# A graph layer and a routed expert layer on one core: the loop's squares move to ScalarE, the degree guard to a spare tile row, one-hots to five places, and the end of the routing is put in another order

## What is computed

```python
def gnn(feat, W_self, W_neigh, b, src, dst):      # feat = layernorm(x)
    agg = segment_sum(feat[src], dst, n)          # 53125 edges, sorted by dst
    deg = segment_sum(ones, dst, n)
    return feat @ W_self + (agg / max(deg, 1)) @ W_neigh + b

def ffn(x, ...):                                  # x = layernorm(x1)
    vals, idx = top_k(x @ gate_w + gate_b, 2)
    h = relu(x @ w1[e] + b1[e]); y_e = h @ w2[e] + b2[e]      # for the two experts
    return layernorm(x + sum_k softmax(vals)_k * y_idx_k) * gamma + beta

x1 = x + gnn(layernorm(x), ...)
out = x1 + ffn(layernorm(x1), ...)
```

## Time and profile before

| | us |
|---|---|
| median of 3 runs | 567.57 (565.23 to 568.28) |
| the profiled execution | 565.0 |
| its span, first to last instruction | 563.1 |

### The profile page before, as it was taken

The page is one execution under the profiler, slowest core; times in us unless marked ns, Lnnn a source line. Parts: engine busy times, 40 slices in busy tenths (PEclk is TensorE's granted clock), DMA queues, the critical chain, the costliest instruction groups (busy, mean ns, idle before and its releaser), DMA issues.

```text
span 563.1 us, 14414 instructions
## 1 busy us (share of the span) xinstructions
PE 479.7 (85%) x5119; PEld 410.8 (73%) x5119; DVE 439.1 (78%) x1090; ACT 379.5 (67%) x929; POOL 339.7 (60%) x479
## 2 busy tenths in 40 slices
PE   1899989999898998999934799999999999998820
PEld 0455568887787886888824698899999999896610
DVE  4888769999998999989865777676777777664794
ACT  1455656877775876866643588888888888877131
POOL 5672007777665677577410677777777777652383
PEclk9999989999998999999966799999999999999975
DMA  9410024444543344321130423632332222337989
GB/s 217 96 29 1 1 78 124 135 118 128 146 122 101 114 136 122 91 70 38 31 119 1 122 73 112 170 94 79 96 92 87 74 82 81 72 90 186 220 131 147
DMA packets 45077, 56.68 MB, mean 101 GB/s; under 512 B 5347, under 2 KB 37851, under 8 KB 45006
## 3 DMA queue, kind: packets, MB, share of 16 engines
q1 hardware_dynamic: 34736, 36.73, 24.3%
q0 software_dynamic: 9440, 18.28, 13.0%
q10 hardware_dynamic: 830, 0.74, 0.6%
HBM read 39.73 MB, written 17.99 MB: 102 GB/s over the span
## 4 chain that ended last, share of the span: by engine, by line
PE 49%; DVE 31%; DMA 7%; issue 5%; POOL 3%; ACT 2%; SPq 1%; DVEq 0%; ACTq 0%; POOLq 0%
PE PS L1251 13%; PE PS L1263 13%; DVE W L1405 7%; DVE W L1498 5%; PE PS L1064 4%; PE PS L1144 4%; PE PS L1145 4%; DVE oh_extra L1405 3%; PE PS L1096 3%; DMA W<-z_tab 2%; DMA arena<-xh_tab,tok_of 2%; PE PS L1239 2%; DVE AGG L1506 2%; DVE arena L1508 1%; DVE AGG L1586 1%
## 5 line engine op out<-in xcount | busy, mean ns | idle before, releaser
L1144 PE MATMUL PS<-arena,AGG 125*128 125x257 f16 x625 | 148.9, 276 | 0.0
L1145 PE MATMUL PS<-arena,AGG 125*128 125x256 f16 x625 | 148.4, 274 | 0.0
L850 ACT ACTIVATE AGG<-PS 128x500 f16<-128x500 f32 (+1 forms) x175 | 93.1, 542 | 39.6 <-PE PS L1096 36.3
L1251 PE MATMUL PS<-arena,AGG 128*128 128x128 f16 x1536 | 97.9, 221 | 1.7 <-issue 0.8
L752 POOL DMA_INDIRECT z_tab<-arena,meta_of x64 | 79.9, 1249 | 31.5 <-issue 19.5
L1263 PE MATMUL PS<-AGG,arena 128*128 128x256 f16 x768 | 95.8, 273 | 1.3 <-DVE AGG L1714 1.0
L1251 PEld LDWEIGHTS PS<-arena,AGG 128*128 128x128 f16 x1536 | 89.9, 99 | 2.9 <-DVE AGG L1708 1.6
L746 POOL DMA_INDIRECT arena<-xh_tab,tok_of x64 | 66.8, 1044 | 37.0 <-issue 17.8
L980 ACT ACTIVATE arena<-PS,arena 128x128 f32<-128x128 f32 x256 | 73.2, 369 | 10.4 <-PE PS L1251 4.0
L1263 PEld LDWEIGHTS PS<-AGG,arena 128*128 128x128 f16 x768 | 72.8, 98 | 10.1 <-DVE AGG L1714 1.2
L1405 DVE TENSOR_TENSOR W<-table,arena 128x1024 f16<-128x1024 f16 x104 | 74.7, 727 | 6.6 <-PE PS L1096 6.6
(11 more groups left out here) (243 smaller groups left out, 890.3 us busy)
## 6 DMA issues: line engine op xcount, KB each, us to landing
W<-in_L_ffn_w SPq DMA_DIRECT2D x60, 256.0 KB, 3.2
out<-AGG SPq DMA_DIRECT2D x25, 125.0 KB
xh_tab<-arena SPq DMA_DIRECT2D x25, 125.0 KB
W<-z_tab SPq DMA_DIRECT2D x2, 1344.0 KB
W<-z_tab SPq DMA_DIRECT2D x2, 896.0 KB
W<-in_x SPq DMA_DIRECT2D x2, 784.0 KB
AGG<-out SPq DMA_DIRECT2D x2, 672.0 KB
out<-W POOLq DMA_DIRECT2D x2, 672.0 KB, 6.9
```

The source lines that it names most:

```text
L850: a.activation(AT[j % 2][:, :, QT * GD * s:QT * GD * s + n * GD].rearrange("p h (g l) -> p h g l", l=GD), (p_A0[s % 2] if j == 0 else p_A[ ...
L1144: t.matmul(p_agg[j % 2], AT[j % 2][0:BT, h, :], HW[0:BT, h, D:HS - 1], start=(h == 0), stop=False)
L1145: ins = t.matmul(p_agg[j % 2][:, 0:D], AT[j % 2][0:BT, h, :], HW[0:BT, h, 0:D], start=False, stop=(h == NB - 1))
L1251: ins = t.matmul(p_h[s % 2][:, c * P:(c + 1) * P], w1e[:, s % 2, wa, k, c * P:(c + 1) * P], xT[:, s % 2, xa, k, :], start=(y == 0), stop=( ...
```

## The change

Its edits fall in four groups.

- **Squares on ScalarE.** For row blocks 0 to 22, `x1_norm` ends with the fused operation that makes x1 and also sums it (`accum_out`). GpSimd makes minus the mean from the sum. ScalarE squares x1 minus the mean with an accumulated sum (`x1_square`, new, behind evict 3 of the pass behind). GpSimd does the rest of the scale from that. Statistics and aggregate go from VectorE for these rows. ScalarE's order in a pass becomes: weight, evict 0, xt_make, evict 1, xt_high, weight, evict 2, xtT_out, evict 3, x1_square, weight, evicts 4 to 6.
- **Degree guard.** Row 125 of the count tile and of `HW` holds 2^-14 (written by GpSimd in the prologue), the degree column holds 16, and one step of the degree's product reads 126 rows. The maximum with 1 goes from `x1_norm`; its reciprocal reads PSUM.
- **Five places.** One-hots have five places up to batch 113 (the first of pass 18's block), three after. The two new ones lie where the last expert's second weights go; SyncE waits for 452 products before the load that uses that room for staging.
- **Routing end.** Row one-hots are laid out with the two choices next to each other. TensorE multiplies two chunks before it transposes the item list. ScalarE makes the last expert's high halves before it scales the last set, and VectorE their low halves before it reads the gather's result.

```diff
@@ -26,7 +26,9 @@
-ORING = 3
+ORING = 5
+ORING_LATE = 3
+SHRINK_AT = -(-BG * 18 // QT)
...
+        def hot_place(q):
+            return q % ORING if q < SHRINK_AT else (q - SHRINK_AT) % ORING_LATE
+        def hot_before(q):
+            return max([r for r in range(q) if hot_place(r) == hot_place(q)], default=-1)
@@ -598,6 +614,8 @@
+                if n + STAGES == NPIECE:
+                    sp.wait_ge(tiles_done, QT * SHRINK_AT)
@@ -691,6 +709,13 @@
+            pool.wait_ge(consts_made, 15)
+            g.memset(HW[96:P, 0, 0:2 * D], 0.0).then_inc(guarded, 1)
+            g.memset(HW[96:P, 0, 2 * D:HS], GUARD).then_inc(guarded, 1)
+            for v in range(2):
+                g.memset(AT[v][96:P, 0, 0:BT], GUARD).then_inc(guarded, 1)
+            pool.wait_ge(guarded, 4)
...
-            g.memset(HW[:, :, 2 * D:HS], 1.0).then_inc(cleared, 1)
+            g.memset(HW[0:BT, :, 2 * D:HS], WSS).then_inc(cleared, 1)
@@ -756,16 +782,18 @@
-                y, m = rstds[:, j:j + 1], mv[:, j % 2, :]
-                pool.wait_ge(mv_made, j + 1)
-                link(g.tensor_scalar(sc[0], m[:, 1:2], EPS, None, ALU.add))
+                y, nm = rstds[:, j:j + 1], x1_nmean[:, j % 2:j % 2 + 1]
+                pool.wait_ge(x1_made, j + 1)
+                g.tensor_scalar(nm, x1_sum[:, j % 2:j % 2 + 1], -1.0 / D, None, ALU.mult).then_inc(x1_mean, 1)
+                pool.wait_ge(x1_squared, j + 1)
+                link(g.tensor_scalar(sc[0], x1_sq[:, j % 2:j % 2 + 1], 1.0 / D, EPS, ALU.mult, ALU.add))
...
-                link(g.tensor_tensor(sc[1], m[:, 0:1], y, ALU.mult))
-                g.tensor_scalar(nmr[:, j % 2:j % 2 + 1], sc[1], -1.0, None, ALU.mult).then_inc(x1_scaled, 1)
+                pool.wait_ge(x1_mean, j + 1)
+                g.tensor_tensor(nmr[:, j % 2:j % 2 + 1], nm, y, ALU.mult).then_inc(x1_scaled, 1)
@@ -870,21 +898,32 @@
+            def x1_square(j):
+                act.wait_ge(x1_mean, j + 1)
+                if j >= 2:
+                    act.wait_ge(x1_scaled, j - 1)
+                    act.wait_ge(xtT_made, j)
+                    act.wait_ge(xt_lo, j - 1)
+                a.activation(xt_of(j), x1_of(j), ACT.Square, bias=x1_nmean[:, j % 2:j % 2 + 1],
+                             accum_out=x1_sq[:, j % 2:j % 2 + 1]).then_inc(x1_squared, 1)
@@ -927,18 +966,20 @@
             for i in range(NB):
-                if i >= 2:
-                    xt_make(i - 2)
                 weight_high(slot_piece(i, 0))
                 A_evict(i + 1, 0)
                 if i >= 2:
+                    xt_make(i - 2)
+                A_evict(i + 1, 1)
+                if i >= 2:
                     xt_high(i - 2)
                 weight_high(slot_piece(i, 1))
-                A_evict(i + 1, 1)
                 A_evict(i + 1, 2)
                 if i >= 2:
                     xtT_out(i - 2)
                 A_evict(i + 1, 3)
+                if 1 <= i < NB - 1:
+                    x1_square(i - 1)
...
-            scale_tokens(SETS - 1)
-            scale_blocks(SETS - 1)
             for c, (w, src_f, scale) in enumerate(((W1, wstg4, WS1), (W2, wstg3, WS2))):
                 act.wait_ge(last_loaded, 2 * DMA)
                 a.activation(w[:, NEXP - 1, 0, :, :].rearrange("p k f -> p (k f)"), src_f, ACT.Copy, scale=scale).then_inc(last_hi, 1)
+            scale_tokens(SETS - 1)
+            scale_blocks(SETS - 1)
@@ -1141,7 +1182,8 @@
-                    t.matmul(p_agg[j % 2], AT[j % 2][0:BT, h, :], HW[0:BT, h, D:HS - 1], start=(h == 0), stop=False)
+                    rows = BT + 1 if h == 0 else BT
+                    t.matmul(p_agg[j % 2], AT[j % 2][0:rows, h, :], HW[0:rows, h, D:HS - 1], start=(h == 0), stop=False)
@@ -1215,8 +1257,6 @@
-            pe.wait_ge(item_cols, 1)
-            t.transpose(p_item, scr[0:NITEM, 0:1], ident[0:NITEM, 0:NITEM]).then_inc(item_T, 1)
...
                 ins.then_inc(chunk_done, 1)
+                if c == 1:
+                    pe.wait_ge(item_cols, 1)
+                    t.transpose(p_item, scr[0:NITEM, 0:1], ident[0:NITEM, 0:NITEM]).then_inc(item_T, 1)
@@ -1399,10 +1442,10 @@
-                if q >= ORING:
-                    dve.wait_ge(tiles_done, QT * (q - ORING + 1))
+                if hot_before(q) >= 0:
+                    dve.wait_ge(tiles_done, QT * (hot_before(q) + 1))
@@ -1501,16 +1544,18 @@
-                link(v.tensor_scalar(deg[:, 0:1], p_deg[j % 2], 1.0, WSS, ALU.max, ALU.mult))
-                link(v.reciprocal(deg[:, 1:2], deg[:, 0:1]))
-                v.scalar_tensor_tensor(x1, p_x1[j % 2], deg[:, 1:2], own[:, j, :], ALU.mult, ALU.add).then_inc(x1_made, 1)
-                dve.wait_ge(x1_made, j + 1)
-                link(v.bn_stats(stats, x1))
-                if j >= 2:
-                    dve.wait_ge(x1_scaled, j - 1)
-                v.bn_aggr(mv[:, j % 2, :], stats).then_inc(mv_made, 1)
-                if is_late(j):
-                    dve.wait_ge(mv_made, j + 1)
+                link(v.reciprocal(deg[:, 1:2], p_deg[j % 2]))
+                if not is_late(j):
+                    if j >= 2:
+                        dve.wait_ge(x1_mean, j - 1)
+                    v.scalar_tensor_tensor(x1, p_x1[j % 2], deg[:, 1:2], own[:, j, :], ALU.mult, ALU.add,
+                                           accum_out=x1_sum[:, j % 2:j % 2 + 1]).then_inc(x1_made, 1)
+                else:
...
@@ -1581,10 +1626,10 @@
-                v.tensor_tensor(row_blk[:, bs, :, :], iota16[0:BT, :].unsqueeze(1).unsqueeze(1).to_broadcast([BT, SETB, 2, P]),
-                                row16[:, :, 0:2].unsqueeze(3).to_broadcast([BT, SETB, 2, P]), ALU.is_equal).then_inc(rows_hot, 1)
+                v.tensor_tensor(row_blk[:, bs, :, :], table[0:BT, :, 0:2].unsqueeze(1).to_broadcast([BT, SETB, P, 2]),
+                                row16.unsqueeze(2).to_broadcast([BT, SETB, P, 2]), ALU.is_equal).then_inc(rows_hot, 1)
@@ -1664,6 +1709,10 @@
+            for c, (w, src_f, scale) in enumerate(((W1, wstg4, WS1), (W2, wstg3, WS2))):
+                dve.wait_ge(last_hi, c + 1)
+                whl = w[:, NEXP - 1, :, :, :].rearrange("p a k f -> p a (k f)")
+                v.scalar_tensor_tensor(whl[:, 1, :], src_f, scale, whl[:, 0, :], ALU.mult, ALU.subtract).then_inc(last_lo, 1)
```

More of the change, by code:

```diff
@@ L43 @@
 NITEM = NEXP + (2 * N - NEXP) // P
+GUARD = 2.0 ** -14
 SKIP = 1 << 20
@@ L213, in build @@
         nmr = part(2)[0:BT, :]
+        x1_sum, x1_nmean, x1_sq = [part(2)[0:BT, :] for _ in range(3)]
         sc = [part(1)[0:BT, :] for _ in range(2)]
@@ L384, in build @@
         cleared = sem("cleared")
+        guarded = sem("guarded")
         x_loaded = [sem(f"x_loaded{c}") for c in range(NPRO)]
@@ L420, in build @@
         x1_made = sem("x1_made")
+        x1_mean = sem("x1_mean")
+        x1_squared = sem("x1_squared")
         mv_made = sem("mv_made")
@@ L849, in A_evict @@
                     act.wait_ge(agg_done, j - 1)
-                a.activation(AT[j % 2][:, :, QT * GD * s:QT * GD * s + n * GD].rearrange("p h (g l) -> p h g l", l=GD),
-                             (p_A0[s % 2] if j == 0 else p_A[(BQ * j + s) % 4])[:, 0:n * BT].rearrange("p (g h l) -> p h g l", h=NB, l=GD), ACT.Copy).then_inc(A_out, 1)
+                a.activation(AT[j % 2][0:BT, :, QT * GD * s:QT * GD * s + n * GD].rearrange("p h (g l) -> p h g l", l=GD),
+                             (p_A0[s % 2] if j == 0 else p_A[(BQ * j + s) % 4])[0:BT, 0:n * BT].rearrange("p (g h l) -> p h g l", h=NB, l=GD), ACT.Copy).then_inc(A_out, 1)
             for k in range(max(NB + 3, BUILD_AFTER + 2 + BQ)):
@@ L895, in scale_tokens @@
                 for k in range(2):
-                    ins = a.activation(row_tok[:, bs, k, :], row_blk[:, bs, k, :], ACT.Copy, scale=tok2[:, k:k + 1])
+                    ins = a.activation(row_tok[:, bs, :, k], row_blk[:, bs, :, k], ACT.Copy, scale=tok2[:, k:k + 1])
                 ins.then_inc(rows_scaled, 1)
@@ L1094, in build_quad @@
                     r, w = divmod(u, PAIR)
-                    hot = oh[q % ORING]
+                    hot = oh[hot_place(q)]
                     t.matmul(to[:, c * BT:(c + 1) * BT], hot[:, r, :, w], hot[:, QT // PAIR + r, 0:BT, w],
@@ L1675, in _ @@
             v.scalar_tensor_tensor(meta_of[:, 0:NITEM], slot_id, -2.0 * BT - 1.0, skip, ALU.add, ALU.add).then_inc(meta_of_made, 1)
-            for c, (w, src_f, scale) in enumerate(((W1, wstg4, WS1), (W2, wstg3, WS2))):
-                dve.wait_ge(last_hi, c + 1)
-                whl = w[:, NEXP - 1, :, :, :].rearrange("p a k f -> p a (k f)")
-                v.scalar_tensor_tensor(whl[:, 1, :], src_f, scale, whl[:, 0, :], ALU.mult, ALU.subtract).then_inc(last_lo, 1)
             def gate_rows(part):
```

32 lines of the change are left out of this document (20 added, 12 removed).

## The result

The changed kernel took 552.2 us, the median of four runs (548.5, 550.3, 554.2 and a disturbed one of 1244.2, without which it is 550.3), against 566.5 for the kernel before (565.2 to 568.3); without that run the ratio is 0.971, with an interval of 0.966 to 0.976. A second set gave 551.6 against 567.6, ratio 0.974 (0.968 to 0.980). The forecast was 559.0, a gain of 8.7 us; the gain is 14 to 16.

What follows compares the result with a forecast made beforehand. The prediction took VectorE as the bound with a GpSimd-ScalarE ring of equal length beneath, the ring setting the pass after the change. Loop 4.7 plus end 4.0 gave 8.7 us: 567.6 to 558.9, say 559; range 549 to 571.

Steps and rivals of the forecast that it cites:

- the loop: The 22 passes from row 0's normalisation to row 22's: forecast at 8.2 us each, 180.4 in all, a gain of 4.7 us.
- the signs that were to show it right: VectorE idle over 1 us a pass, row-scale ends 8.2 us apart, first gather product some 3 us earlier, one table load.
- the ring's sum: Turn length in the loop: 7.97 - 0.45 + 0.60 + 0.15 + 0.08 + 0.2 = 8.55 us, before credit for idle VectorE.
- the ring: GpSimd's row scale, ScalarE's xt and high half, GpSimd's beta and low half, next row scale: claimed to set the pass.
- the relief that idle VectorE gives GpSimd: GpSimd's small steps take 0.19 us, not 0.52, without VectorE's one-hots: credited 0.2 us in routing-free passes, 0.45 in others.
- xt_make's move: In ScalarE's pass, xt_make behind the first weight piece and eviction: GpSimd waits less for the high half, -0.45 us a turn.
- VectorE's terms: In the loop: normalisation 0.74 us less a pass, three row one-hots 0.7 less each; demand 7.12 us a pass.
- The routing end: Serial work behind the loop: 1.1 us from the last set and late normalisations, 2.9 from earlier tokens, 4.0 in all.
- Rival 1: In the loop TensorE becomes the bound, as GpSimd gains more from idle VectorE than credited: 550 us, chance 0.18.
- Rival 2: In the loop the ring takes what VectorE gives, 8.55 us a turn without relief: 566.6 us, no difference, chance 0.22.
- Rival 3: In the loop the ring grows further, as operations taken from VectorE are those beside which GpSimd runs fast: 574, chance 0.13.
- Rival 4: On ScalarE the square is not among the loaded functions, two table loads a pass add 59 us: some 618, chance 0.02.

## Why the prediction was right or wrong

The direction and the two places of the gain were right. The size was not: the loop was to give 4.7 us and gave 9.0 to 9.3. The whole difference lies in passes 1 to 7. The forecast had them at 8.35 us each, 58.5 in all, longer than the 55.9 before; they took 54.5 and 54.3. The other fifteen were to take 8.1 each, 121.5, and took 121.6. Of the signs that were to show it right, VectorE's idle time was 0.58 us a pass and not over 1, and the ends of the row scale lay 7.99 us apart as a mean of all 22 turns, not 8.2.

**The step that failed** is the ring's sum, and with it the claim that the ring sets the pass. The parts of a turn, as means of the first six turns from the timelines of GpSimd and ScalarE:

| part of a turn, us | before | forecast | changed |
|---|---|---|---|
| square and read-out | none | +0.75 | +0.60 |
| waits between the first step, the square and the rest | 0.08 | +0.28 | 0.31 (+0.23) |
| beta step to low half, xt_make moved | 0.44 | -0.45 | 0.27 (-0.17) |
| seven steps behind the first (and the square) | 4.24 | -0.20 | 3.56 (-0.68) |
| turn | 7.97 | 8.35 | 7.77 |

The rest of the difference lies in the beta step and low half (0.91 and 0.96 before, 0.81 and 0.90 after) and in minus the mean, which starts 0.11 us sooner behind the low half than the first step did.

I had named the relief that idle VectorE gives GpSimd and credited 0.2 us for it in the first passes; it was 0.68, and 0.56 between the second executions of the two kernels. I sized it by how long VectorE would stand still, as if that were an outcome of the two engines' loads. The runs show that it answers to the ring: longer by two steps, the ring pays 0.78 of 1.1 us; later by one weight piece, VectorE waits twice as often. The other mis-sized terms were smaller and partly cancelled. The largest is xt_make's move: its 0.45 came from the wait's mean over all rows, while in the turns that the sum starts from the whole wait was 0.44, and 0.27 of it stayed.

So short a ring is not the bound by itself. It is of nearly one length with TensorE in the first seven passes: cut either and little happens, cut both and 2.5 us go; lighter work on VectorE, which also shortens GpSimd's steps (3.27 us there), gave 1.0 to 1.1 alone. In the other fifteen the forecast's 8.1 us was right for a wrong reason: a shorter ring left them at 122.1, and VectorE's relief brought them to 116.5. Since one engine's added work is paid only in part (VectorE's 12.9 us cost 6.2 to 6.5), no single engine's busy time gives the pass.

**VectorE's terms.** The normalisation went from 1.46 to 0.61 us, 0.85 less and not 0.74; the read-out was 0.08 as taken. The row one-hot took 0.83 (0.82 said), and three of them gave 2.1 us in the loop, as said. But VectorE's busy time fell to 163.3 us, not to 156. The larger part of that miss is the low halves, which grew by 74 ns each, 4.4 us in 60; two small routing operations grew by 1.2 together. I had priced the contention of VectorE and GpSimd on GpSimd's side alone. By the timelines of the changed kernel a low half takes 1.15 us on average (0.92 to 1.22) where one of GpSimd's two operations of 256 elements had begun ahead of it and still had over 0.1 us to run (16 of 60; 7 of 60 before the change). The other 44 took 0.69, beside nothing, beside a small step, or, in four places, beside such an operation that began behind them. One place of either kind, from the timelines of both engines:

```profile
139.32 1.22 DVE L1541 SCALAR_TENSOR_TENSOR W<-W 128x512 f16<-128x512 f32 x1
...
147.27 0.68 DVE L1541 SCALAR_TENSOR_TENSOR W<-W 128x512 f16<-128x512 f32 x1
```

```profile
139.19 0.80 POOL L801 TENSOR_TENSOR AGG<-AGG,beta_b 125x256 f32<-125x256 f32 x1 [0.95 <-ACT arena L927]
140.12 0.91 POOL L803 TENSOR_TENSOR arena<-arena 125x256 f16<-125x256 f32 x1
...
147.44 1.09 POOL L801 TENSOR_TENSOR AGG<-AGG,beta_b 125x256 f32<-125x256 f32 x1 [0.71 <-ACT arena L927]
```

The Trainium skill, SBUF — State Buffer, "Who interferes with whom", has a VectorE instruction with two SBUF inputs contend with a GpSimd instruction that reads SBUF, and one with at most one, outside the modes that use two ports, not. The traces agree on both halves: GpSimd's small steps took 0.52 beside one-hots and 0.19 beside the fused operation, which takes one tensor from PSUM and one from SBUF (13 of them). The page also says that it is the order of issue that decides who is held up. The two places above agree: VectorE took 1.22 us behind GpSimd's operation and 0.68 ahead of it, where GpSimd's took 1.09 instead of 0.80.

**Five places.** I gave them nothing while another bound holds; they gave 1.9 us alone and 1.2 to 1.4 with the rest. A bound on the mean pass says nothing of waits that come from uneven passes. These are what went: VectorE's waits for a free place fell from 6.7 us in the kernel before to 1.8 with the places alone, and they are 2.1 us in the changed kernel where they are 5.5 with three places.

**The degree guard** cost nothing that shows: its fills stand in the prologue, and start to row 0 is 82.5 to 83.6 us against 83.2 to 84.0.

**The routing end** was to give 4.0 us and gave 3.5 to 3.7: 0.4 from the late normalisations as said, 3.4 from the new order and the row one-hot, where 3.6 were said. Counted from row 22, the first gather product stood 3.9 us ahead of the transpose's place before (28.2 and 32.1 us, "some 3"), and the last low halves were covered. What I missed is ScalarE's scaling of the paired layout, 1.91 for two against 1.55; the last ten products wait for it, by 0.20 us.

**The rivals.** Rival 1 had nearly the time (550) and half the mechanism: TensorE holds the first seven passes, but together with the ring, and VectorE holds the others. Rival 2 credited no relief; in no run was the mean of the first six turns as long as its 8.55 (8.13 at most). Rival 3's price did not come: taking the statistics from VectorE made GpSimd's steps shorter, and putting them back made them longer (3.56 to 4.02). Rival 4 is out by the one table load of 1.28 us. The Trainium skill, ScalarE: Activation LUTs, "Table sets: the hidden batching unit", has relu, copy, identity and abs in every set; here the square, too, ran under the one load that serves copy, identity, relu and the exponential.

## What to carry to other kernels

Where two engines slow each other, the length of a ring through one of them is no constant to add to: whatever holds the ring up idles the other engine and shortens it again, so test which bound holds by cutting it, not by adding its parts. Where a stage's busy times stand within a few per cent of each other, cut the candidates one at a time and then two together: bounds of equal length hide each other, and a cut that brings nothing alone shows little about either. When work leaves an engine that contends, price the contention on both sides, and look at which operations a moved step will then run beside.

## What the runs showed of the hardware

ScalarE's read-out of an accumulated sum takes 0.20 us (200 ns mean of 23), against VectorE's 0.08; begun before the square's record ends, it makes a square of 125x256 with its sum 0.60 us. A ScalarE copy of 125x640 float16 elements that reads and writes every second element took 1.02 us, against 0.82 for one that takes them in runs of 128 (medians of ten in the changed kernel and in the one before).

With 29 us less to do, TensorE ran at a lower granted clock: 0.92 and 0.90 as means of passes 8 to 22 in the two kernels with fewer products, 1.00 in the changed kernel. That is a mean between its levels of 1.2 and 2.4 GHz, so for a part of these passes it ran at the lower one. What it did before: in the first of the two the clock was at full level until 134.2 us and fell there. Up to that time, in passes 1 to 7, TensorE had waited 11.3 us in 15 stretches for VectorE's one-hots; in the same passes of the changed kernel, where it did not fall, it was 1.6 in 3.
